# Decoder layer: the next batch's scores between the last P.V and the output product, its query product in steps 2 and 3, its maxima ahead of the norm

## The reference

```python
x = x + attn(layernorm(x))            # causal self-attention, 32 query heads, 8 key heads, head size 16, RoPE
x = x + xattn(layernorm(x), ctx)      # cross-attention over 128 context rows and the latents, 32 heads of 128
x = x + ffn(layernorm(x))             # relu^2 FFN and a routed low-rank path
# attn, per batch:
q, k, v = x @ Wq.T, x @ Wk.T, x @ Wv.T
q, k = rope(q), rope(k)
p = softmax(mask(q @ k.T / sqrt(16)))
out = (p @ v) @ Wo.T
```

## Time and profile before

| | us |
|---|---|
| median of 3 runs | 1110.77 (1110.03 to 1111.12) |
| the profiled execution, its own time | 1113.87 |
| its span in the profile | 1112.1 |
| PE busy | 1041.2 (94%) |
| DVE busy | 642.6 (58%) |
| ACT busy | 544.0 (49%) |
| POOL busy | 388.7 (35%) |

### The profile page before, as it was taken

How to read it: one execution, slowest core, us unless ns; L and a number is a source line. 1 busy time by engine, 2 the same in 40 slices (tenths; PEclk the granted TensorE clock), 3 DMA queues, 4 the chain that set the end, 5 groups by cost and what they waited for, 6 DMA issues and landing times.

```text
span 1112.1 us, 19290 instructions
## 1 busy us (share of the span) xinstructions
PE 1041.2 (94%) x6808; PEld 922.9 (83%) x6808; DVE 642.6 (58%) x1369; ACT 544.0 (49%) x1657; POOL 388.7 (35%) x370
## 2 busy tenths in 40 slices
PE   5888988889889999998999998999999999999997
PEld 5666766666568899998999997999999999899996
DVE  5677777777742555553555554555556556645554
ACT  4556654565542554653645543545546446632121
POOL 2444444434440432431623422424415225621110
PEclk9999999999999999999999999999999999999999
DMA  9211110010428110311202121111312022300000
GB/s 322 84 31 39 39 34 19 25 39 20 131 56 268 39 39 29 105 58 40 58 19 86 48 76 49 35 43 58 104 35 62 20 77 85 96 20 19 19 19 19
DMA packets 70123, 68.64 MB, mean 62 GB/s; under 512 B 3984, under 2 KB 53904, under 8 KB 70032
## 3 DMA queue, kind: packets, MB, share of 16 engines
q1 hardware_dynamic: 70032, 67.43, 19.6%
HBM read 48.55 MB, written 18.87 MB: 61 GB/s over the span
## 4 chain that ended last, share of the span: by engine, by line
PE 75%; DVE 13%; ACT 6%; issue 3%; POOL 2%; DMA 1%; DVEq 0%; SPq 0%; POOLq 0%; ACTq 0%
PE bank L218 22%; PE bank L220 22%; PE bank L219 22%; PE bank L923 4%; ACT Pa L1086 3%; DVE PTal L1278 2%; DVE Kbdl L1369 2%; DVE a_nb L1394 1%; PE bank L711 1%; POOL Pa L505 1%; ACT PTah L1031 1%; DVE b_nb L1506 1%; ACT Pb L1168 1%; DVE b_max L1503 1%; PE bank L605 1%
## 5 line engine op out<-in xcount | busy, mean ns | idle before, releaser
L541 POOL TENSOR_TENSOR Pb<-Pb,b_rec 128x512 f32<-128x512 f32 x128 | 133.3, 1042 | 408.1 <-DVE b_rec L1510 407.8
L218 PE MATMUL bank<-XTh,WQh 128*128 128x256 f32 x512 | 147.0, 287 | 3.8 <-DVE Ql L1278 3.8
L219 PE MATMUL bank<-XTl,WQh 128*128 128x256 f32 x512 | 145.7, 285 | 0.0
L220 PE MATMUL bank<-XTh,WQl 128*128 128x256 f32 x512 | 145.7, 284 | 0.0
L1168 ACT ACTIVATE Pb<-bank,b_nb 128x256 f32<-128x256 f32 x256 | 119.2, 471 | 30.1 <-DVE b_nb L1506 29.2
L1031 ACT ACTIVATE PTh<-bank 128x512 fp32r<-128x512 f32 x128 | 76.8, 600 | 107.5 <-PE bank L923 107.4
L1086 ACT ACTIVATE Pa<-bank,a_nb 128x128 f32<-128x128 f32 x256 | 91.7, 392 | 66.6 <-DVE a_nb L1394 66.6
L1278 DVE TENSOR_TENSOR Ol<-bank,Oh 128x256 fp32r<-128x256 f32 x128 | 53.7, 420 | 117.5 <-ACT Oh L1031 117.5
L218 PE MATMUL bank<-WOh,Oh 128*128 128x512 f32 x256 | 110.4, 431 | 1.0 <-DVE x_res L1520 1.0
L218 PEld LDWEIGHTS bank<-XTh,WQh 128*128 128x128 f32 x512 | 98.6, 193 | 9.2 <-DVE Ql L1278 4.8
L219 PEld LDWEIGHTS bank<-XTl,WQh 128*128 128x128 f32 x512 | 98.7, 193 | 4.6
(11 more groups left out here) (230 smaller groups left out, 2881.7 us busy)
## 6 DMA issues: line engine op xcount, KB each, us to landing
kv_scratch<-KVst SPq DMA_DIRECT2D x64, 256.0 KB, 3.0
KV<-kv_scratch SPq DMA_DIRECT2D x32, 512.0 KB, 3.4
raw<-in_L_xattn_Wo_dram SPq DMA_DIRECT2D x32, 256.0 KB, 3.3
raw<-in_L_xattn_Wq_dram SPq DMA_DIRECT2D x24, 256.0 KB, 4.1
cx<-in_ctx_dram SPq DMA_DIRECT2D x8, 256.0 KB, 8.8
raw_first<-in_L_xattn_Wq_dram SPq DMA_DIRECT2D x8, 256.0 KB, 4.7
raw<-in_L_ffn_up_w_dram SPq DMA_DIRECT2D x8, 256.0 KB, 4.3
raw<-in_L_ffn_down_w_dram SPq DMA_DIRECT2D x8, 256.0 KB, 2.7
```

What stands on the lines that cost most here:

```text
L218: pe.matmul(dst, lh, rh, start=start, stop=False)
L219: pe.matmul(dst, lh, rl, start=False, stop=False)
L220: return pe.matmul(dst, ll, rh, start=False, stop=stop)
L541: gp.tensor_tensor(pk, pk, b_rec[:, k % 4, :].unsqueeze(2).to_broadcast([P, 2, KEYS]), ALU.mult).then_inc(b_g_norm, 1)
```

## The change

On PE, `scores(b + 1, 0)` moves from behind the output product to the front of it, `scores(b + 1, 1)` from behind the latents' transposes to right behind the product. In the steps, scores 2 and the transposes of xn go to step 0 (the latter from step 1), scores 3 to step 3, the two halves of the query product from steps 3 and 4 to 2 and 3, and the key and value product from steps 5 and 6 to 4. On ACT, exponentials run three steps ahead of the eviction instead of two, and stand behind it. On DVE the maxima of the next batch move ahead of the residual and the norm, the statistics and the norm xn of the batch after next go to steps 1 and 2, and the rotation comes in steps 3 to 5. On POOL normalisation 0 and 1 of the next batch surround the last key tile and rstd.

The same in the diff, cut to its core:

```diff
 POOL   def batch(b, last):
-                if not last:
-                    inv_std1(b + 1)
                 for j in range(2, SKV):
                     normalise(b, j)
+                    if j == 3 and b + 2 < NB:
+                        inv_std1(b + 2)
                 if not last:
-                    diagonal_keys(b + 1, range(KC))
+                    diagonal_keys(b + 1, range(3))
+                    normalise(b + 1, 0)
+                    diagonal_keys(b + 1, (3,))
...
                 gp.tensor_tensor(rstd[:], var_eps[:], half[:], ALU.pow).then_inc(g_rstd, 1)
                 if not last:
-                    normalise(b + 1, 0)
                     normalise(b + 1, 1)
...
 PE     for j in range(SKV):
                     turn(j)
-                    if j in (1, 3):
-                        scores(b, (j + 3) // 2)
                     if j == 0:
...
                         unit(U_B0 + 2 * b)
-                    if j == 5 and not last:
-                        kv_product((0, 1))
-                    if j == 6 and not last:
-                        kv_product((2, 3))
+                        if not last:
...
+                            turn_xn(b + 1)
+                        scores(b, 2)
+                    if j == 2 and not last:
...
+                        q_product((0, 1))
+                    if j == 3:
+                        scores(b, 3)
+                        if not last:
+                            q_product((2, 3))
+                    if j == 4 and not last:
+                        kv_product(range(KC))
                     if j == 7 and not last:
                         turn_qk(b + 1)
                     if j >= 1:
                         values(j - 1)
-                    if j == 1 and not last:
...
-                        turn_xn(b + 1)
-                    if j == 3 and not last:
...
-                        q_product((0, 1))
-                    if j == 4 and not last:
-                        q_product((2, 3))
                 values(SKV - 1)
+                if not last:
+
+                    pe.wait_ge(a_exp, SKV * b + SKV)
+                    scores(b + 1, 0)
+
...
                 op.then_inc(pe_wo, 1)
                 if not last:
-
-                    pe.wait_ge(a_exp, SKV * b + SKV)
-                    scores(b + 1, 0)
+                    scores(b + 1, 1)
                 unit(U_B0 + 2 * b + 1)
...
                 turn_latents(b)
-                if not last:
-                    scores(b + 1, 1)
...
 ACT    for j in range(SKV):
-                    if j + 2 < SKV:
-                        probs(b, j + 2)
                     act.wait_ge(pe_pt, SKV * b + j + 1)
                     hi(PTah[:, j % 2, :], bank[5 + j % 2][:]).then_inc(a_pt, 1)
-                    if j == 1:
+                    if j + 3 < SKV:
+                        probs(b, j + 3)
+                    if j == 0:
                         unit_hi(U_B0 + 2 * b)
-                    if j == 2 and not last:
-                        xn_hi(b + 1)
+                        if not last:
+                            xn_hi(b + 1)
...
                     values_hi(b + 1)
+                    for j in range(3):
+                        probs(b + 1, j)
...
-                if not last:
-                    probs(b + 1, 0)
-                    probs(b + 1, 1)
                 unit_hi(U_B0 + 2 * b + 1)
...
 DVE    for j in range(SKV):
...
-                    if j == 0 and not last:
-                        ln1(b + 1)
                     if j + 2 < SKV:
                         reciprocals_a(b, j + 2)
-                    if j == 1:
+                    if j == 0:
                         unit_lo(U_B0 + 2 * b)
                     if last:
                         continue
-                    if j == 2:
+                    if j == 0:
                         ln1_lo(b + 1)
+                    if j == 1 and b + 2 < NB:
+                        ln1_stats(b + 2)
+                    if j == 2 and b + 2 < NB:
+                        ln1(b + 2)
+                    if j == 3:
+                        rope_q(b + 1)
+                    if j == 4:
+                        rope_k_parts(b + 1)
                     if j == 5:
-                        rope_q(b + 1)
-                    if j == 6:
-                        rope_k(b + 1)
+                        rope_k_sum(b + 1)
...
                 if not last:
+                    maxima(b + 1, 0)
                     diagonal_keys(b + 1, (1,))
+                    maxima(b + 1, 1)
                     values_lo(b + 1)
+                    reciprocals_a(b + 1, 0)
 
                 dve.wait_ge(pe_wo, b + 1)
...
                 norm_stats(x_res[:, b, :], v_st2)
                 if not last:
-                    maxima(b + 1, 0)
-                    maxima(b + 1, 1)
+                    reciprocals_a(b + 1, 1)
+                    maxima(b + 1, 2)
...
                 if not last:
-                    reciprocals_a(b + 1, 0)
-                    reciprocals_a(b + 1, 1)
                     diagonal_keys(b + 1, (2, 3))
                 unit_lo(U_B0 + 2 * b + 1)
                 latents_lo(b)
-                if not last:
-                    maxima(b + 1, 2)
-                if b + 2 < NB:
-                    ln1_stats(b + 2)
```

More of the change, by code:

```diff
@@ L533, in _ @@
                     normalise(0, kc // 2)
+            inv_std1(1)
             for b in range(NB):
@@ L742, in batch @@
                         unit(U_B0 + 2 * b)
-                    if j == 5 and not last:
-                        kv_product((0, 1))
-                    if j == 6 and not last:
-                        kv_product((2, 3))
+                        if not last:
+                            if b:
+                                pe.wait_ge(v_htl, b)
+                            else:
+                                pe.wait_ge(v_ctl, 6)
+                            turn_xn(b + 1)
+                        scores(b, 2)
+                    if j == 2 and not last:
+                        pe.wait_ge(v_xnl, b + 2)
+                        pe.wait_ge(v_ul, U_B0 + 2 * b + 1)
+                        q_product((0, 1))
[5 more added lines that the diff above has]
+                        kv_product(range(KC))
                     if j == 7 and not last:
@@ L750, in batch @@
                         values(j - 1)
-                    if j == 1 and not last:
[L753 to L756, removed]
-                        turn_xn(b + 1)
-                    if j == 3 and not last:
-                        pe.wait_ge(v_xnl, b + 2)
-                        pe.wait_ge(v_ul, U_B0 + 2 * b + 1)
-                        q_product((0, 1))
-                    if j == 4 and not last:
-                        q_product((2, 3))
                 values(SKV - 1)
+                if not last:
+                    pe.wait_ge(a_exp, SKV * b + SKV)
+                    scores(b + 1, 0)
                 for g in range(SG):
@@ L1156, in _ @@
             unit_hi(4)
+            probs(0, 2)
             for b in range(NB):
@@ L1318, in ln1 @@
                 dve.wait_ge(g_rstd1, b + 1)
+                if b:
+                    dve.wait_ge(pe_xn, b)
                 dve.tensor_scalar(xn[:], x_res[:, b, :], mv1[:, 0:1], rstd1[:], ALU.subtract,
@@ L1343, in rope_q, with rope_k_parts, rope_k_sum @@
                 dve.tensor_tensor(q_rot[:], rope_q1[:], rope_q2[:], ALU.add).then_inc(v_qr, 1)
-            def rope_k(b):
+            def rope_k_parts(b):
                 dve.wait_ge(pe_qkv, 2 * b + 2)
                 rotate(bank[0][:, 0:P], rope_k1[:], rope_k2[:], 1, SKV, 0)
+            def rope_k_sum(b):
                 dve.wait_ge(v_rt, 6 * b + 6)
@@ L1470, in _ @@
             rope_q(0)
-            rope_k(0)
+            rope_k_parts(0)
+            rope_k_sum(0)
             unit_lo(0)
@@ L1493, in _ @@
                 context_lo(b)
+            ln1(1)
             unit_lo(4)
```

## The result

| | before | after |
|---|---|---|
| median, us | 1110.4 (1109.97 to 1111.12, 4 runs) | 1090.63 (1088.76 to 1091.63, 4 runs) |
| profiled execution, us | 1113.87 | 1089.78 |
| its span, us | 1112.1 | 1088.1 |

The ratio is 0.9817 with a 95% interval of 0.9802 to 0.9832. That is 20.3 us faster, between 18.7 and 22.0 (the two medians are 19.8 apart). Forecast were 1088.9 us and 21.9 less.

A forecast was written before the change was run, and what follows sets the result against it. PE was taken to bound the kernel, busy 94%, with 4.24 us idle per full batch. Gains of 18.9 + 1.5 + 1.5 = 21.9 us from 1110.8 gave 1088.9 us, range 1080.5 to 1098.5.

The forecast's parts named there:

- Boundary: From transpose 7 to the next batch's transpose 0: 12.4 us instead of 15.07, a gain of 2.7 per batch.
- Scores 0 wait for KTl: At the boundary, before scores 0: PE idles 0.6 us until DVE has KTl at 3.2 after transpose 7.
- xn2 meets normalisation 1: At the boundary, DVE's xn2 beside POOL: takes 1.48 us, costs nothing by 0.1, up to 0.5 if slower.
- Steps: From transpose 0 to transpose 7 of a batch: 19.25 us instead of 19.73, a gain of 0.5.
- The block behind the rotation: Step 3 on DVE: query rotation holds about 2.0 us with maxima 7 queued behind; P.V 5 late by 0.5, transpose 7 by 0.4.
- kr meets normalisation 7: Late steps: DVE's sum kr starts 0.15 before POOL's normalisation 7, which takes 1.40 instead of 1.04; +0.36, bounds 0 and 0.69.
- Last batch: Transpose 7 comes 16.55 us after transpose 0 instead of 18.05, a gain of 1.5.
- Sum: Whole kernel: full batch 31.65, gain 3.15, six times 18.9, plus 1.5 first and 1.5 last batch: 21.9 us.
- PE hardly waits any more: Rival, chance 0.10: a full batch costs only PE's busy time, 30.56 us; gain 29.9, or 1080.9 us.
- Behind it all stays: Phases after the last batch's self-attention: bound by PE, they only shift and do not change in time.
- The slower rival: Chance 0.05: exponentials 0 come no earlier, scores 1 start at 13.2 instead of 7.6; batch 37.2, about 1128 us.
- The sum by the rule: Shared-port rule at kr and normalisation 7: whoever starts second is blocked, +0.5 instead of +0.36, whole prediction about 1 us later.

The follow-up runs named there:

- the kernel with the keys split: Against the change: maxima 7 in step 3, PE's split wait, key product halved into steps 4 and 5, key rotation in step 5; 1080.76 us.
- the kernel with maxima 7 first: Against the change: DVE's maxima 7 moved into step 3, ahead of the query rotation; 1089.2 us, 0.9801 of the kernel before.
- the kernel with kr in step 6: Against the change: DVE's sum kr moved to step 6, PE waiting for q_rot and kr separately; 1089.99 us, 0.9808 of the kernel before.
- the kernel with the maxima behind: Against the change: DVE's maxima 0, maxima 1 and reciprocal 0 put back behind the residual and its statistics; 1137.4 us, 1.0235 of the kernel before.
- kr in step 4: Against the change: DVE's sum kr moved to step 4, right behind the other rotation parts; 1089.75 us, 0.9800 of the kernel before.

## Why the prediction was right, point by point

- *Boundary.* Forecast 12.4, measured 12.54, at all seven boundaries within 0.01. The wait for OTl lies under scores 0, scores 1 do not wait, the latents do not wait. Scores 0 start 3.42 after transpose 7 where 3.2 was walked, and from there to the next transpose 0 it is 9.12 where 9.2 was walked. The lateness begins with q_rot's transposes, 0.50 behind transpose 7 instead of 0.35; why is not shown, for it is 0.50 too in the kernel with the keys split, where the rows show no wait for transpose 7.
- *Scores 0 wait for KTl.* Forecast 0.6; the bracket is 0.48, and from start to start it is 0.64.
- *xn2 meets normalisation 1.* Forecast 1.48 and no cost by 0.1; it took 1.25 and had 0.2 to spare.
- *Steps.* Forecast 19.25, measured 19.43. The forecast had P.V 5 late by 0.5, and transpose 7 by 0.4 and by 0.36 for the collision. To lay rows beside it, take the starts, with 0.35 for a transposed tile and 0.80 for P.V where nothing is late. P.V 5 starts 0.95 after transpose 6, so it is late by 0.6, and transpose 7 starts 1.56 after that, so it is late by 0.76. Transpose 6 starts 1.49 after transpose 5 where 1.1 was walked: it waits for normalisation 6, which the walk did not have. Transpose 5 in turn comes 15.44 after transpose 0 where 15.7 was walked. That the two nearly cancel (0.4 later, 0.26 sooner) is luck. The block behind the rotation was named, and the kernel with maxima 7 first shows it: 0.43.
- *kr meets normalisation 7.* Forecast 1.40 for the normalisation, measured 1.40; undone by the kernel with kr in step 6, 0.37.
- *Last batch.* Forecast 16.55, measured 16.55.
- *Sum.* From the first transpose 0 to the last transpose 7 it was 260.03 and is 240.32 (50.57 to 290.89): 19.7 less, where 21.9 were forecast. Seven times 0.31 are the missing 2.2: the term that was mis-sized is the full batch, 31.65 against 31.96.
- *PE hardly waits any more* was priced by a floor that is none. It took PE's busy time in a full batch, 30.56, for what is left without waits. The same matmuls are 30.39 busy in the change, and the kernel with the keys split takes 30.48 for a whole batch, wait included, with 29.98 of it busy. The records show why: the four transposes of a tile have 0.60, yet the next matmul starts 0.35 after their start where nothing waits; in front of a wait the whole 0.60 or 0.66 counts as busy. So a bracket is smaller than the time that its wait costs: 0.30 for the 0.6 at P.V 5.
- *Behind it all stays.* From the last transpose 7 to the end the stretch is 799.7 before and 797.2 after, and 798.1 with the change run again; the start ended at 52.40, 50.57 and 51.68. The nine other kernels, whose phases there are those of the change, give 796.9 to 799.0. So some 4 us of the difference between the two profiled executions lie outside the batches, and at least 2 of them are chance, since the change run again has them back; whether the rest is cannot be told from one trace of the kernel before. The medians, 19.8 apart, agree with the self-attention alone.
- *The slower rival* had the chain right. It has PE wait 5.6 in front of scores 1 (13.2 less 7.6) and a batch of 37.2. The kernel with the maxima behind comes nearest: its wait is 4.19, which alone would give some 36.2 (19.4, and 12.1 of work and 4.7 of idle time). It takes 37.9 to 39.5, since the clock falls. That loss stands nowhere in the prediction, and it makes the rival's price too low.
- *What I wrote on the shared port.* The sum by the rule, +0.5, is the whole rest of kr: 0.66 less the 0.16 between the two starts. Measured is +0.36, which is what the sum went by. The half-sentence on the row of 1.40 gave the key tile 0.6 that it did not have: it too starts 0.16 ahead of the normalisation, and a key tile takes 0.69 where nothing holds it up (201.17 in the new trace), so that 0.5 was left. The row is the very geometry of kr and normalisation 7, and so its 0.36 could be carried over as it was. The row of 1.48 fits the rule less well than I wrote: POOL's first operation had some 1.28 left (half of 2.69, less 0.07), and xn2 grew by 0.94 over the 0.54 that it takes alone.

DVE's rows before, the norm xn2 alone and the pair of key tiles that the normalisation at 224.57 meets:

```profile
221.85 0.54 DVE L1445 TENSOR_SCALAR xn<-x_res,mv,rstd 128x512 f32<-128x512 f32 x1
...
224.41 2.11 DVE L1369 TENSOR_TENSOR Kbdl<-KTl,bd_mask 128x512 fp32r<-128x512 f32 x2
```

## What to carry to other kernels

A wait that ends a chain over three engines is not worth its bracket. Lay the whole loop out once with the durations of the old trace, and look at what stands in front of the chain's first link on each engine. Here scores 0 moved up without DVE's maxima made the kernel 2.4% slower than before, the maxima moved up without scores 0 made it 1% slower, and both together 1.8% faster. Part of the two losses is the clock; without it they would still be about 0.9% and 0.4% (estimates, with the time above a clock of 1.00 taken off, 16.8 and 6.2 us).

Measure a wait of PE from start to start, against the same pair of blocks where nothing waits. The bracket leaves out the end of the matmuls before it, so neither the sum of the brackets nor the busy time is what can be won.

Once the large waits are gone, read who is second in each meeting of DVE and POOL, and which instruction is queued behind one that waits. And give the steps whose chain is longer than PE's work a piece of independent work, in halves if need be (0.7 us per batch here).

## What the hardware showed that I had not expected

Where DVE and POOL meet, the one issued second pays, and the first takes what it takes alone. In the change kr is first, at 196.25; normalisation 7, issued 0.16 later, takes 1.40 instead of 1.04. With kr in step 4 the normalisation is first and takes 1.04; kr, issued 0.40 later, takes 1.20 instead of 0.66, and the kernel with the keys split makes use of that. The Trainium skill says this of such a pair ("SBUF — State Buffer", Who interferes with whom): a DVE instruction with two SBUF inputs contends with a GpSimd instruction that reads SBUF, over a port pair that is an exclusive lock, and the order of issue decides who is blocked. The rows agree on who pays. The price is a little under what the first has left: 0.36 for 0.50 left, and 0.54 for 0.64.

The norms xn and xn2, which have one full input and two single columns, meet POOL in the same way. The normalisation at 220.23 pays 0.21 for 0.35 left; xn2 at 208.50 pays 0.71 (1.25 for 0.54) for 0.97, and ends 0.28 after the normalisation. In these four meetings the price is 0.10 to 0.26 us less than the rest; where the difference comes from was not tried.

The same wait of 2.32 us, behind the same work, left the granted clock at 1.00 in three boundaries and brought it to 0.90 in four, for 1.56 us each; the wait of 4.19 brought it down each time, to 0.82 to 0.91 of the boundary. There the seven boundaries come in a pattern of three: 19.04, 18.51 and 20.02 us, then 19.16, 18.52 and 20.07, then 19.18. In the change, with waits of at most 0.60, and in the kernel before, with waits of up to 1.56, the clock is 1.00 in every batch. What decides between the three and the four was not tried.
